# A graph layer's second bias by a TensorE product, unread products in the refinement's waits, and a third norm sum in late tridiagonal steps

## What is computed

```python
deg = jnp.sum(A, axis=0) + jnp.sum(A, axis=1) - jnp.diagonal(A)
d_inv_sqrt = jnp.where(deg > 0, jax.lax.rsqrt(deg), 0.0)
L_norm = d_inv_sqrt[:, None] * (jnp.diag(deg) - A) * d_inv_sqrt[None, :]
_, U = jnp.linalg.eigh(L_norm)
agg = jnp.einsum('mn,bnd->bmd', U.T, features)
h = jax.nn.relu(agg @ W1 + b1)
out = h @ W2 + b2
return jnp.einsum('nm,bmd->bnd', U, out)
```

## Time and profile before

| | |
|---|---|
| time, median of 3 runs | 1321.49 us (1317.4 to 1322.62) |
| the profiled execution | 1331.45 us, span 1329.7 us |
| PE busy | 1103.1 us (83%) |
| PEld busy | 928.6 us (70%) |
| DVE busy | 917.3 us (69%) |
| ACT busy | 567.4 us (43%) |
| POOL busy | 505.9 us (38%) |
| mean granted clock of PE | 0.944 |

### The profile page before, as it was taken

One profiled execution on the slowest core, in us unless ns is written; L12 is line 12 of the kernel. 1 busy time (PEld: TensorE's weight loads), 2 busy tenths in 40 slices (PEclk: granted clock), 3 DMA queues, 4 the chain that ended last, 5 costly groups with the idle time before them and its releaser, 6 DMA issues.

```text
span 1329.7 us, 25184 instructions
## 1 busy us (share of the span) xinstructions
PE 1103.1 (83%) x7028; PEld 928.6 (70%) x7028; DVE 917.3 (69%) x3880; ACT 567.4 (43%) x1722; POOL 505.9 (38%) x556
## 2 busy tenths in 40 slices
PE   4555655557874999999999999798889999999996
PEld 3555544546652888978889754376667999889994
DVE  5777689858885666756667587768753667656683
ACT  2556654514541222212222257556534444444452
POOL 2200000024675444434444352004763555545551
PEclk9999999758875999999999989899999999999998
DMA  9999995000223444314332260001223444143326
GB/s 186 403 430 427 427 430 243 1 0 12 82 85 105 132 127 129 109 55 115 97 88 80 61 228 1 17 1 57 89 86 117 141 150 124 57 130 107 105 63 196
DMA packets 78874, 182.66 MB, mean 137 GB/s; under 512 B 11752, under 2 KB 51699, under 8 KB 75408
## 3 DMA queue, kind: packets, MB, share of 16 engines
q0 software_dynamic: 20544, 112.80, 21.4%
q1 hardware_dynamic: 58192, 68.27, 19.1%
HBM read 65.10 MB, written 119.08 MB: 139 GB/s over the span
## 4 chain that ended last, share of the span: by engine, by line
PE 62%; DVE 21%; issue 10%; ACT 3%; POOL 1%; DMA 1%; SPq 1%; another core or an unknown queue 0%; DVEq 0%; POOLq 0%; ACTq 0%
PE bank L1709 18%; PE bank L1695 17%; PE bank L1698 7%; PE bank L198 4%; PE bank L1935 3%; PE bank L1928 3%; PE bank L1681 2%; PE bank L1862 2%; DVE work L333 1%; DVE u L330 1%; PE bank L1443 1%; DVE u L183 1%; PE bank L895 1%; DVE bnh L1763 1%; DVE u L174 1%
## 5 line engine op out<-in xcount | busy, mean ns | idle before, releaser
L1695 PE MATMUL bank<-work,wide 128*128 128x256 f32 (+3 forms) x994 | 215.4, 330 | 3.7 <-issue 1.9
L1709 PE MATMUL bank<-wide,work 128*128 128x128 f32 x1512 | 216.4, 278 | 0.4 <-DVE work L1625 0.2
L1709 PEld LDWEIGHTS bank<-wide,work 128*128 128x128 f32 x1512 | 197.9, 191 | 9.7 <-DVE work L1625 3.6
L1653 ACT ACTIVATE work<-bank 128x256 f32<-128x256 f32 (+1 forms) x216 | 82.7, 383 | 261.5 <-PE bank L1698 233.6
L1038 POOL DMA_INDIRECT rows<-tokens,slot x128 | 125.2, 978 | 129.2 <-issue 48.5
L1695 PEld LDWEIGHTS bank<-work,wide 128*128 128x128 f32 (+1 forms) x994 | 154.1, 186 | 16.7 <-DVE wide L1561 2.8
L1540 POOL DMA_INDIRECT rows<-wide x100 | 104.1, 1041 | 122.1 <-DVE wide L1577 101.9
L198 PE MATMUL bank<-u 63*64 63x2 f32 (+61 forms) x496 | 73.7, 255 | 66.3 <-DVE u L183 65.2
L1625 DVE TENSOR_TENSOR work<-work,bank 128x256 f32<-128x256 f32 (+1 forms) x216 | 88.1, 417 | 41.3 <-ACT work L1653 38.5
L198 PEld LDWEIGHTS bank<-u 63*64 63x64 f32 (+61 forms) x496 | 64.4, 217 | 71.7 <-DVE u L183 70.4
L1561 DVE COPY wide<-wreg 128x1066 f32 (+1 forms) x142 | 100.8, 710 | 19.3 <-issue 15.1
(11 more groups left out here) (445 smaller groups left out, 2396.6 us busy)
## 6 DMA issues: line engine op xcount, KB each, us to landing
rows<-wide POOLq DMA_DIRECT2D x20, 3432.0 KB, 110.0
wide<-rows SPq DMA_DIRECT2D x100, 260.0 KB
wide<-rows SPq DMA_DIRECT2D x88, 130.0 KB
wreg<-in_w SPq DMA_DIRECT2D x1, 4264.0 KB, 37.7
wreg<-in_w SPq DMA_DIRECT2D x1, 4112.0 KB, 14.3
tokens<-in_x SPq DMA_DIRECT2D x2, 2048.0 KB, 20.5
tokens<-in_xt SPq DMA_DIRECT2D x1, 4096.0 KB, 41.9
tokens<-plane SPq DMA_DIRECT2D x16, 256.0 KB, 5.4
```

What stands on the lines that cost most here:

```text
L1653: A.activation(t["hs"][c][0:w, :], ps[c][0:w, 0:TS], ACT.Silu).then_inc(s("hs"), 1)
L1695: ins = T.matmul(ps[c][0:n, to], w[:, a:a + n], x[:, to], start=True, stop=True)
L1709: ins = T.matmul(ps[4 + j % 2][:, h * P:(h + 1) * P], t["hh"][c][0:n, h * P:(h + 1) * P], w[0:n, at + c * P:at + (c + 1) * P], start=(c == ...
```

## The change

Three edits.

- **Norm sums.** `SUMS_FROM` is 8, the step from which there were two sums already. From `THIRD_FROM`, 42, on a third one stands at the end of each step. So 128 of the 129 calls are in the reduction, and one is left for the first pass of the sections.
- **Unread products.** One `keep_warm` product ahead of each wait for `e_ready` (three rounds), and one ahead of the wait for `ut_ready`.
- **Bias.** PE multiplies `UTB` with `b2row` (b2 repeated in all partitions) into the same bank as the product with U, and that adds to it. It stands ahead of the wait for ACT's copy (`a0_gm`), but behind the wait for DVE's addition two tiles back (`a0_xadd`), which frees the bank. PE's product for the row sums of U, DVE's copy of them, GpSimd's multiplication and 16 additions, and DVE's wait for these, are gone.

```diff
-EARLY_SUMS = 108
+SUMS_FROM, THIRD_FROM = 8, 42
+EARLY_SUMS = 2 * (STEPS - SUMS_FROM) + STEPS - THIRD_FROM
...
-        if k >= STEPS - EARLY_SUMS // 2:
+        if k >= SUMS_FROM:
             first_norm_sum(nc, act, S, E, t, sums)
             sums += 1
...
         F.activation(m["VRT"][0:n, 0:n], VR[0:n, 0:n], ACT.Copy, scale=c[0:n, 6:7]).then_inc(ha, 1)
-        if k >= STEPS - EARLY_SUMS // 2:
+        if k >= SUMS_FROM:
+            first_norm_sum(nc, act, S, E, t, sums)
+            sums += 1
+        if k >= THIRD_FROM:
             first_norm_sum(nc, act, S, E, t, sums)
             sums += 1
...
         mm(ps[5][0:N, 0:N], ones[:, 0:N], m["sq2"][:, :]).then_inc(*E.on(f"srow_ready{r}"))
+        keep_warm(nc, t, ps[3], 1)
         pe.wait_ge(*E.at(f"e_ready{r}"))
...
     mm(ps[0][0:N, 0:N], m["X"][:, :], m["Q"][:, :]).then_inc(*E.on("w_ready"))
+    keep_warm(nc, t, ps[3], 1)
     pe.wait_ge(*E.at("ut_ready"))
...
-    T.matmul(ps[7][:, 0:1], t["UTB"], t["ones"][:, 0:1], start=True, stop=True).then_inc(S("a0_rows"), 1)
...
         if 0 <= s < TILES:
-            pe.wait_ge(S("a0_gm"), s + 1)
             if s >= 2:
                 pe.wait_ge(S("a0_xadd"), s - 1)
-            T.matmul(ps[(3, 6)[s % 2]][:, :], t["UTB"], t["gm"][s % 2], start=True, stop=True).then_inc(S("a0_out"), 1)
+            T.matmul(ps[(3, 6)[s % 2]][:, :], t["UTB"], t["b2row"], start=True, stop=False)
+            pe.wait_ge(S("a0_gm"), s + 1)
+            T.matmul(ps[(3, 6)[s % 2]][:, :], t["UTB"], t["gm"][s % 2], start=False, stop=True).then_inc(S("a0_out"), 1)
...
-    dve.wait_ge(S("a0_rows"), 1)
-    V.tensor_copy(t["rows"], ps[7][:, 0:1]).then_inc(S("a0_rows_out"), 1)
...
-            dve.wait_ge(S("a0_pre"), s)
...
-    pool.wait_ge(S("a0_rows_out"), 1)
-    pool.wait_ge(S("small_in"), 16)
-    nc.gpsimd.tensor_scalar(t["b2mixed"], t["b2row"], t["rows"], None, ALU.mult).then_inc(S("a0_b2"), 1)
-    pool.wait_ge(S("a0_b2"), 1)
-    pool.wait_ge(S("l1_done"), N)
-    for T in range(TILES):
-        xt = t["X"][:, T * PAIRS:(T + 1) * PAIRS, :]
-        nc.gpsimd.tensor_tensor(xt, xt, pairs(t["b2mixed"]), ALU.add).then_inc(S("a0_pre"), 1)
```

More of the change, by code:

```diff
@@ L2230, in build @@
         t["tb"]["cmp"] = take(2 * E8 * 32)
-        t["b2mixed"], t["rows"] = work[:, 0:TOK], take(1)
         u = [U1[:, k * TOK:(k + 1) * TOK] for k in range(16)]
```

## The result

The changed kernel takes 1323.44 us (median of 22 runs, 1320.42 to 1324.97), the kernel before 1318.56 us beside it (22 runs, 1316.03 to 1324.18). The ratio is 1.0026, 95% interval 1.0016 to 1.0035: **slower by 0.26%, some 3.4 us**. I had forecast 1317.3 us, a gain of 4.2. The profiled execution of the changed kernel took 1322.41 us.

A forecast was written before the change was run, and what follows sets the result against it. DVE's chain paced the reduction and refinement; group 0's start and GpSimd's pace set the first stage's end. Sums -1.2, unread products 0 and first stage -3.0 made -4.2 us: 1321.49 to 1317.3, range 1311.5 to 1323.5.

The forecast's parts named there:

- The wait for the join should fall from 2.10 to the 0.86 us: First section pass: DVE's wait for the joining product shrinks once the sums leave, -1.24 us.
- I take -1.2: Norm sums moved from the first section pass into ACT's idle time: -1.2 us, bounds 0 and -1.24.
- Unread products at 0: Refinement and last wait: the unread products fit PE's pauses with 0.6 and 0.35 us slack, cost 0.
- Group 0's sends start 0.5 us earlier: First stage: GpSimd's first sends at 327.4, not 327.93; the added product eats the rest of DVE's freed 6 us.
- After that three loops are level: PE 11.98, DVE 12.10, GpSimd 12.2 us per group: First stage after group 0: each engine's own loop nearly equal, so groups follow at GpSimd's 12.2 us.
- the term of -3.0 us: First stage: group 7's sends start at 412.8 instead of 415.83, 0.5 us of it from the early start.
- a forecast of 85: First stage: 85 us between the first sends of groups 0 and 7, not 87.9.
- What follows moves as a block: Behind the first stage: last eight sends, warm-up products and experts shift together, so the stage's gain reaches the end.
- The base: Whole kernel: median before of 1321.49 us, to which the differences from the profiled 1331.45 us were carried unchanged.
- Rival B: Refinement: unread products raise the clock before the first stage begins, 1314.5 us, total -7.0; chance 0.25.
- Rival C: First stage: PE becomes the bound, clock falls as often, 12.8 us per group, 1321.6 us, no change; chance 0.22.
- Rival D: First stage: clock at half for 30% of the ramp, 13.9 us per group, about 1329.5 us, slower; chance 0.08.

The follow-up runs named there:

- experiment 12: Kernel before with the cheap bias, third norm sums and seven unread products behind 760 us, none in the refinement: 1314.82 us, ratio 0.9959 to the kernel before.
- 2: Kernel before with only the third norm sums added: 1318.84 us, ratio 1.0002 (0.999 to 1.0015).
- 14: Kernel before, cut short behind layer 0's first stage, with the bias edit alone: 447.37 us.
- 6: Changed kernel, cut short behind layer 0's first stage: 448.10 us, against 446.25 for the kernel before cut the same way.
- experiment 9: Kernel before with seven unread products in three PE pauses behind 760 us (the filled kernel before): 1317.91 us.
- experiment 1: Kernel before, unchanged, executed once more for a second trace (the second execution of before): 1320.49 us.
- the cheap product: bf16 product of constant 1/64 with the bias, opening the second layer's bank, replacing GpSimd's additions in the kernel before: 0.21 us each.
- the early count: Counting products issued ahead of the product with U (and any fp32 bias product): short changed kernel 442.19 us, whole changed kernel 1316.28, kernel before 1317.37.
- the cheap bias: Kernel before with the second bias by a bf16 product on PE, GpSimd's additions gone: 443.18 us cut short, 1319.94 whole.
- experiments 7 and 8: Kernel before with the cheap bias: cut short behind layer 0's first stage 443.18 us against 446.25; whole 1319.94 us, ratio 1.0007.
- experiments 9 to 11: Seven unread products in pauses behind 760 us, added to the kernel before, the changed kernel and the cheap bias: 1317.91, 1320.55 and 1316.29 us.
- the short kernel: Kernel ending behind layer 0's first stage, writing out the tokens: before 446.25 us, changed 448.10, changed with the early count 442.19.
- the filling: Seven unread 128x512 products in three PE pauses behind 760 us; added to the kernel before they gave 1317.91 us.
- experiment 11: Kernel before with the cheap bias and seven unread products in pauses behind 760 us: 1316.29 us.
- filled changed: Changed kernel with seven unread products in pauses behind 760 us: 1320.55 us.

## Why the prediction was wrong

- *"The wait for the join should fall from 2.10 to the 0.86 us"*: right, 0.89, and the steps' period didn't change. *"I take -1.2"* for the whole kernel: seen as -1.5 in experiment 12, as nothing in 2 and in 14 against 6. Between 0 and -1.5; open.
- *Unread products at 0*: right (0.9997). They left 0.41 us of their slack.
- *"Group 0's sends start 0.5 us earlier"*: right in size, 0.6 beside the sums, though profiles of kernels that are the same up to there start group 0 anywhere from 326.44 (experiment 9) to 328.74 (experiment 1). That the freed DVE gains little because the added product eats it was right too: the cheap product brings the whole 5 us.
- ***"After that three loops are level: PE 11.98, DVE 12.10, GpSimd 12.2 us per group"* is the step that failed.** I had counted loops engine by engine and left out the one that crosses them, DVE 6.0 + PE 6.5 = 12.5 us. PE's pieces were in the earlier trace rows, and DVE's wait for the count was in the profile of before. PE's sum was right and beside the point: what counted was what stood in PE's queue between the logits and the count. Of the term of -3.0 us, 2.5 were for groups 1 to 7; they came to +1.3 in the profile (415.28 - 326.11 = 89.2 us between the sends of groups 0 and 7, against 87.9 and a forecast of 85). Only the kernels with the early count come near the forecast's 85 us (85.7 to 86.4). Even with that edit the change gives 1.1 us by medians, not 4.2; what became of the other 3 is open.
- *"What follows moves as a block"* failed too: the cheap bias gains 3.1 us in the stage and nothing sure at the end (experiments 7 and 8). How much of the change's own loss (3.4 us by the ratio, 4.9 by medians) arises in the stage isn't resolved: 1.9 by medians, 1.0 by means, with ranges that overlap. Behind the stage about 0.5 us lies at a fixed place of VectorE's program (last section); the rest may go with the falls of the clock in pauses that the edit doesn't touch, as far as experiments 9 to 11 carry.
- *The base*: the median of before was 1318.56 in 22 runs, not the 1321.49 of three; that alone would have put the forecast at 1314.4.
- *Rival B* didn't happen: 0.52 with PE busy for 88% of the stretch. *Rival C* gave nearly the right time (1321.6) and nearly the right group (12.8 us against 89.2 / 7 = 12.7), by luck: it wanted the clock to fall as often as before, and it fell less (0.97 against 0.93). *Rival D* neither.

## What to carry to other kernels

Before calling a stage bound by one engine's sum of work, follow the cycle through all engines for one repeat, with what stands ahead of each hand-over in the in-order queue: a product of 0.86 us that the sum of PE's work can bear made a cycle of 11.6 us into the bound, and moving two small products, 0.4 us together, ahead of it and of the product behind it gave 5 to 6 us back in the short kernel. Ask also how long that cycle is where the clock has fallen: there it can be the bound already. If work has to be added to the path of a small product that another engine waits for, issue the small one first. A gain measured at one stage's end isn't yet a gain at the kernel's end: cut the kernel short, time both, and compare.

## What the runs showed of the hardware

**The clock falls in a pause in one execution and not in the next.** Pauses of 1.64 and 1.01 us ahead of a batch brought a fall, pauses of 1.48 and 1.01 none; in the kernel with the sums alone pauses of 1.56 and 1.01 brought none, in the one with the unread products alone 1.57 and 1.02 brought one. In all, the clock falls between 760 and 775 us in seven of nine profiles without the filling and in none of five with it. Between 845 and 870 us it falls in all nine, and of the five in that of experiment 11 alone (0.57 from 848 to 852 us). So with an unread product in each pause the fall is rare. At the start of the stage the rise came within 293 to 297 us in the traces that I read there, but the mean granted clock of those 4 us is 0.55 in the second execution of before and 0.83 in the changed kernel. The Trainium skill (TensorE: Matmul & The Clock Gate, What's actually happening) says that the point of a transition moves from run to run, depending on where the first product falls. These traces agree that it moves; on what that depends they don't show.

**Keeping PE busy didn't raise the clock** in the refinement: 24.27 of 27.60 us busy at 0.52, where products of 64 columns and unread ones of 512 alternate. No run here shows why.

**VectorE pauses at a fixed place of its program.** Between two copies that wait for nothing, in the filled kernel before and in the filled changed one:

```profile
741.39 0.72 DVE L1561 COPY wide<-wreg 128x1066 f32 x1 [0.15 <-issue]
742.16 0.72 DVE L1561 COPY u<-wreg 128x1066 f32 x1
```

```profile
741.53 0.72 DVE L1555 COPY wide<-wreg 128x1066 f32 x1 [0.15 <-issue]
742.65 0.72 DVE L1555 COPY u<-wreg 128x1066 f32 x1 [0.41 <-issue]
```

PE waits for it later, in the filled changed kernel (in the filled kernel before the same row has no wait):

```profile
743.75 0.71 PE L1703 MATMUL bank<-wide,work 128*128 128x128 f32 x4 [0.37 <-DVE work L1619]
```

I looked for this pause of 0.41 us in the experts of layer 0 in fourteen whole kernels: it is there in all eight without GpSimd's additions, and in none of the six with them. Between two fixed sends of GpSimd around it lie 294.2 to 294.7 us in these (458.25 to 752.84 in the filled changed kernel) and, but for the first profile of before, 293.8 to 294.1 in the others (458.36 to 752.34). VectorE's program is one copy and some waits shorter in these; that this moves the pause was not tried.
